# Values stationary and two heads side by side in the P.V product of two attentions, with 1/Z spread by TensorE

## The reference, cut to what matters

```
q, k, v = xn @ w_q, ctx @ w_k, ctx @ w_v          # per head 256x64, 512x64, 512x64
scores = q @ k.T * scale                          # layer 0: a score of 0 counts as -inf
attn = softmax(scores)                            # 256 x 512 for each batch and head
out = attn @ v                                    # 256 x 64
y = concat(out over 16 heads) @ w_out + b_out     # 256 x 1024 @ 1024 x 128
x = x + y                                         # layer 2: x + tanh(gate) * y
```

## Time and profile before

| | |
|---|---|
| median of 3 runs | 546.78 us (546.55 to 550.07) |
| the profiled execution's span | 545.7 us |
| its own time | not given apart from the span |
| PE, DVE, ACT, POOL busy | 92%, 79%, 63%, 52% |
| PE in P.V (L524) | 65.7 us in 1536 matmuls |
| PE in transposes of P (L509) | 82.0 us in 512 |
| PE in transposes of O (L536) | 10.2 us in 64 |

### The profile page before, as it was taken

How to read it: one execution, slowest core, us unless ns; L and a number is a source line. 1 busy time by engine, 2 the same in 40 slices (tenths; PEclk the granted TensorE clock), 3 DMA queues, 4 the chain that set the end, 5 groups by cost and what they waited for, 6 DMA issues and landing times. The chain is left out here.

```text
span 545.7 us, 13308 instructions
## 1 busy us (share of the span) xinstructions
PE 503.3 (92%) x4905; PEld 289.4 (53%) x4905; DVE 431.3 (79%) x1208; ACT 341.1 (63%) x683; POOL 282.0 (52%) x307
## 2 busy tenths in 40 slices
PE   7889999999899899998998899998999999999996
PEld 3345556667753233343334467635665556954574
DVE  7999999997585888736867899888777777587763
ACT  5698888888247366643762678638888888422212
POOL 7957777777834734400110943227888888400100
PEclk9999999999999899999999899999999999999999
DMA  8660000001130000000000221000000002000000
GB/s 226 141 176 14 1 2 3 1 2 41 40 117 0 2 0 2 3 1 0 2 1 21 78 78 58 2 1 1 2 3 1 1 3 79 2 0 1 2 0 20
DMA packets 24084, 15.43 MB, mean 28 GB/s; under 512 B 8083, under 2 KB 22230, under 8 KB 23894
## 3 DMA queue, kind: packets, MB, share of 16 engines
q1 hardware_dynamic: 24022, 14.60, 9.4%
HBM read 14.33 MB, written 0.26 MB: 27 GB/s over the span
## 5 line engine op out<-in xcount | busy, mean ns | idle before, releaser
L509 PE MATMUL pspair<-ident,PP 128*128 128x128 f32 x512 | 82.0, 283 | 2.0 <-ACT PP L1342 1.8
L509 PEld LDWEIGHTS pspair<-ident,PP 128*128 128x128 f32 x512 | 54.2, 141 | 29.7 <-issue 20.1
L524 PE MATMUL psO<-V,PP 128*128 128x64 f16 x1536 | 65.7, 193 | 2.6 <-DVE Oall L1751 2.0
L524 PEld LDWEIGHTS psO<-V,PP 128*128 128x128 f16 x1536 | 59.9, 98 | 9.1 <-DVE PP L1717 2.9
L1717 DVE TENSOR_TENSOR PP<-pspair,PP 128x512 f16<-128x512 f32 x64 | 44.0, 688 | 25.7 <-ACT PP L1326 25.7
L1405 ACT ACTIVATE PP<-pspair 128x1024 f32<-128x1024 f32 x48 | 46.5, 1021 | 25.4 <-PE pspair L709 25.3
L2401 POOL TENSOR_TENSOR ln_rs<-ln_ve,minus_half 128x4 f32<-128x4 f32 x10 | 10.3, 1032 | 84.2 <-DVE ln_ve L1608 81.0
L1342 ACT ACTIVATE PP<-scores_m,nm 128x512 f32<-128x512 f32 x64 | 46.5, 727 | 5.4 <-DVE nm L1701 5.4
L2412 POOL TENSOR_TENSOR PP<-acc,one 128x512 f16<-128x512 f32 x32 | 33.3, 1040 | 29.3 <-ACT acc L1324 29.3
L2412 POOL TENSOR_TENSOR PP<-y_sb,one 128x512 f16<-128x512 f32 x32 | 33.3, 1040 | 16.9 <-ACT y_sb L1324 16.9
L2415 POOL TENSOR_TENSOR PP<-y_sb,PP 128x512 f16<-128x512 f32 x32 | 37.2, 1161 | 2.5
(11 more groups left out here) (596 smaller groups left out, 1261.2 us busy)
## 6 DMA issues: line engine op xcount, KB each, us to landing
W<-in_L_ffn_W SPq DMA_DIRECT2D x16, 256.0 KB, 2.8
bigw<-in_L_xattn_w_q SPq DMA_DIRECT2D x2, 512.0 KB, 6.4
bigw<-in_L_xattn_w_kv SPq DMA_DIRECT2D x1, 1024.0 KB, 4.7
V<-in_ctx SPq DMA_DIRECT2D x1, 512.0 KB, 4.8
bigw<-in_L_xattn_w_v SPq DMA_DIRECT2D x1, 512.0 KB, 6.2
mask_b<-in_mask_BxS_ff SPq DMA_DIRECT2D x1, 512.0 KB, 7.6
bigw<-in_L_xattn_w_k SPq DMA_DIRECT2D x1, 512.0 KB, 5.8
bigw<-in_L_xattn_w_o SPq DMA_DIRECT2D x1, 512.0 KB, 3.9
```

What stands on the lines that cost most here:

```text
L509: mm = pe.transpose(bank[f"T{j % 2}"][:, k * P:(k + 1) * P], Pb[j % 4][:, k * P:(k + 1) * P], ident[:])
L524: mm = pe.matmul(bank["O"][:, (j % UPH) * a.dv:(j % UPH + 1) * a.dv], (PTH, PTL)[ppart][j % 4][:, k * P:(k + 1) * P], (VH, VL)[vpart][:, b ...
```

## The change

P.V is now computed once for each group, two units after the group's last one (at j%4=2), with the values stationary: for one head a block of 128 keys x 64 value columns is loaded, and the transposed probabilities of both query tiles (256 columns) move. The result has the head's 64 features on the partitions and 256 queries in the columns, so it comes out turned. The two heads of the pair use the lower and the upper 64 columns of the array, and so partitions 0 to 63 and 64 to 127 of bank O; their matmuls alternate (24 matmuls, `values`). The probabilities are kept for eight units in place of four; the further four buffers lie in `bigw`, where the oT buffers were.

1/Z now has to lie along the columns. `factors` makes it with four f32 matmuls for each group, into the other half of bank O: the stationary operand is one column of 1/Z repeated 64 times and the identity moves. ACT copies the result to `RT` (at j%4=3), and DVE multiplies O by RT at j%4=1, straight into `OT` in `Oall`. The transposes of O and the copies behind them are gone.

The output sums of pairs 0 to 5 are taken in the last eight units, one pair with each of j=8 to 13, all four token tiles accumulated in bank M (opened by a matmul of zeros); pair 6 comes behind the last unit, pair 7 in two halves around the last group's P.V, which is taken head by head. The last unit is split by DVE and no longer by POOL. DVE adds y to X in one instruction. Layer 0: the bias and `mask_prep` stand between the last unit's split and the last scaling. Layer 2: the 14 steps of the weight's quantisation and the bias go one by one into the last round's units. POOL's `selectors` wait for the output sums of pair 5.

```diff
-        PT = [PP[:, 4 + k, :] for k in range(4)]
-        PTH = [PT[k][:].bitcast(F16)[:, 0:SK] for k in range(4)]
-        PTL = [PT[k][:].bitcast(F16)[:, SK:2 * SK] for k in range(4)]
+        PT = [PP[:, 4 + k, :] for k in range(4)] + [bigw[:, k // 2, k % 2 * SK:(k % 2 + 1) * SK] for k in range(4)]
+        PTH = [PT[k][:].bitcast(F16)[:, 0:SK] for k in range(8)]
+        PTL = [PT[k][:].bitcast(F16)[:, SK:2 * SK] for k in range(8)]
+        PT_of = [t.rearrange("p a c -> p (a c)").bitcast(F16).rearrange("p (q h m c) -> p h m q c", q=2, h=2, m=2)
+                 for t in (PP[:, 4:8, :], bigw[:, 0:2, :])]
         VH = V[:, 0:4, :].rearrange("p a c -> p (a c)").bitcast(F16).rearrange("p (k c) -> p k c", k=NC)
         VL = V[:, 4:8, :].rearrange("p a c -> p (a c)").bitcast(F16).rearrange("p (k c) -> p k c", k=NC)
...
         minus16 = G[:, 0, 0, :].bitcast(F16)
-        OT = [bigw[:, c // 2, c % 2 * TOK:(c % 2 + 1) * TOK] for c in range(6)] + [kT1[:, 0:TOK], kT1[:, TOK:2 * TOK]]
+        OT = [O[:, (3, 1, 2, 0)[c // 2], c % 2 * TOK:(c % 2 + 1) * TOK] for c in range(NPAIR)]
...
                 mm.then_inc(full[b], 1)
 
-        def out_chunk(j):
-
...
-            def values(i, j):
-
-                if j % 2:
-                    pe.wait_ge(sem(f"{n}.split"), affine(i, j, UPI, 2) + 1)
...
+            def value_part(i, g, h, qs):
+
                 for k in range(a.kt):
+                    for m in range(len(PARTS)):
+                        mm = value_step(i, g, h, qs, k, m)
+                return mm
+
+            def value_step(i, g, h, qs, k, m):
+
+                (ppart, vpart), b, col = PARTS[m], g % B, (PPI * i + g // B) * P + h * DH
+                return pe.matmul(bank["O"][h * DH:(h + 1) * DH, qs.start * P:qs.stop * P]
+                                 .rearrange("p (q x) -> p q x", x=P),
+                                 (VH, VL)[vpart][:, b * a.kt + k, col:col + DH],
+                                 PT_of[g % 2][:, h, ppart, qs, k * P:(k + 1) * P],
+                                 start=(k == 0 and m == 0), stop=(k == a.kt - 1 and m == 2))
+
+            def values(i, g):
+
+                pe.wait_ge(sem(f"{n}.split"), 2 * (i * GPI + g) + 2)
+                emptied(pe, f"{n}.T0", 2 * (i * GPI + g) + 1)
+                reuse(f"{n}.O", i * GPI + g)
+                for k in range(a.kt):
+                    for m in range(len(PARTS)):
+                        for h in range(2):
+                            value_step(i, g, h, slice(0, 2), k, m)
+
+            def factors(i, g, ps, done):
+
+                pe.wait_ge(sem(f"{n}.rz"), i * GPI + g + 1)
+                for q in range(2):
+                    for h in range(2):
+                        mm = pe.matmul(ps[h * DH:(h + 1) * DH, q * P:(q + 1) * P],
+                                       rZ[:, g % 2, 2 * q + h:2 * q + h + 1].broadcast_to([P, DH]), ident[:],
+                                       start=True, stop=True)
+                mm.then_inc(done, 1)
 
             def out_sums(c, ts=range(NT)):
-                emptied(pe, f"{n}.oT{c}")
+
+                emptied(pe, f"{n}.O", B * c + ts[-1] // 2)
                 for t in ts:
-                    out_sum(t, c)
+                    mm = pe.matmul(bank["M"][:, t * P:(t + 1) * P], OT[c][:, t * P:(t + 1) * P], W(c),
+                                   start=False, stop=(c == NPAIR - 1 and t == NT - 1))
+                return mm
...
-                    if not (first and j < a.lag):
-                        values(*shift(i, j - a.lag))
+                    if j % UPH == 2 and not (first and j < UPH):
+                        group = (i, j // UPH - 1) if j >= UPH else (i - 1, GPI - 1)
+                        values(*group)
+                        factors(*group, bank["O"][:, S:2 * S], full["O"])
...
-                    if last and out_chunk(j) is not None:
-                        out_turn(out_chunk(j))
-                    if last and j >= UPI - 3:
-                        if j == UPI - 3:
-                            pe.wait_ge(sem(load), 16)
-                        for c in range(2):
-                            out_sums(c, [j - UPI + 3])
+                    if last and j == UPP:
+                        pe.wait_ge(sem(load), 16)
+                        take(pe, f"{n}.y", "M")
+                        pe.matmul(bank["M"], zero16[:], ident16[:].unsqueeze(1).broadcast_to([P, 4, P]),
+                                  start=True, stop=False)
+                    if last and UPP <= j < UPP + NPAIR - 2:
+                        mm = out_sums(j - UPP)
+                        if a.mask and j == UPP + NPAIR - 3:
+                            mm.then_inc(sem(f"{n}.summed"), 1)
 
...
             run(pe, a, rounds)
-            nr = a.units // UPI
...
+            i, g = a.units // UPI - 1, GPI - 1
+            out_sums(NPAIR - 2)
+            factors(i, g, take(pe, f"{n}.RT", "S0"), full["S0"])
+            reuse(f"{n}.O", i * GPI + g)
+            emptied(pe, f"{n}.T0", 2 * (i * GPI + g) + 1)
+            value_part(i, g, 0, slice(0, 2))
+            pe.wait_ge(sem(f"{n}.split"), 2 * (i * GPI + g) + 1)
+            value_part(i, g, 1, slice(0, 1))
+            out_sums(NPAIR - 1, range(0, 2))
+            emptied(pe, f"{n}.T1", 2 * (i * GPI + g) + 1)
+            value_part(i, g, 1, slice(1, 2)).then_inc(full["O"], 1)
+            out_sums(NPAIR - 1, range(2, 4)).then_inc(full["M"], 1)
...
-                if j % 2:
-                    if not isinstance(i, int) or i * UPI + j >= 4:
+                if not own_low(i, j, a):
+                    if i * UPI + j >= 4:
 
...
-                nc.scalar.copy(PTH[j % 4][:, 0:a.keys], ps[:, 0:a.keys]).then_inc(sem(f"{n}.high"), 1)
+                nc.scalar.copy(PTH[j % 8][:, 0:a.keys], ps[:, 0:a.keys]).then_inc(sem(f"{n}.high"), 1)
+
+            def factors(i, g):
+
+                filled(act, f"{n}.O", i * GPI + g)
+                nc.scalar.copy(RT[:], bank["O"][:, S:2 * S]).then_inc(sem(f"{n}.factors"), 1)
...
+                    if j % UPH == 3 and not (first and j < UPH):
+                        factors(*((i, j // UPH - 1) if j >= UPH else (i - 1, GPI - 1)))
...
             run(act, a, rounds)
+            emptied(act, f"{n}.O", a.units // UPH - 2)
+            act_copy(act, f"{n}.RT", RT[:], S)
...
+                    else:
+                        emptied(dve, f"{n}.RT")
+                    b = g % B
+                    dve.tensor_tensor(OT[PPI * i + g // B][:, b * S:(b + 1) * S], ps[:, 0:S], RT[:], ALU.mult)\
+                        .then_inc(free["O"], 1)
 
                 def rounds(i, first, last):
                     for j in range(UPI):
                         more = not (last and j >= UPP)
                         end = UPI if last else UPI + 4
                         group = (i, j // UPH - 1) if j >= UPH else (i - 1, GPI - 1)
-                        if j % 4 == 3 and not (first and j < UPH):
-                            norm(*group)
+                        if j % 4 == 1 and not (first and j < 2 * UPH):
+                            norm(*((i, j // UPH - 2) if j >= 2 * UPH else (i - 1, GPI - 2 + j // UPH)))
                         if j % UPP == 4 and more:
                             query_low(*pair(i, j // UPP + 1))
                         if a.mask:
@@ -1782,8 +1796,8 @@
                             evac(i, j)
                         if j % UPP == 7 and not last and not a.mask:
                             key_low(*pair(i, j // UPP + 2))
-                        if last and out_chunk(j) in a.dve_turns:
-                            copy(f"{n}.oT{out_chunk(j)}", OT[out_chunk(j)])
+                        if last and j < len(steps):
+                            steps[j]()
 
                 if a.mask:
...
-                norm(*group)
+                i = a.units // UPI - 1
+                recip(i, GPI - 1)
+                norm(i, GPI - 2)
+                evac(i, UPI - 1)
+                for step in behind:
+                    step()
+                norm(i, GPI - 1)
 
             def packed(a, last=(), behind=()):
...
-                weights[-1]().then_inc(sem("L2f.wq"), 1)
-                dve.wait_ge(sem("L2f.wq"), 1)
-                dve.wait_ge(sem("L2x.tanh"), 1)
-                link(dve.scalar_tensor_tensor(out=X[:], in0=wide(rowp["L2_xattn_b_out"]), scalar=tanh_g[:], in1=X[:],
-                                              op0=ALU.mult, op1=ALU.add))
-                for t in range(NT):
-                    ps = filled(dve, f"L2x.y{t}")
-                    dve.scalar_tensor_tensor(out=X[:, t, :], in0=ps[:, 0:P], scalar=tanh_g[:], in1=X[:, t, :],
-                                             op0=ALU.mult, op1=ALU.add).then_inc(free_of(f"L2x.y{t}"), 1)
-                for t in range(NT):
-                    emptied(dve, f"L2x.y{t}")
+                def with_bias():
+                    dve.wait_ge(sem("L2f.wq"), 1)
```

(21 more changed lines are left out.)

102 lines of the change are left out of this document (23 added, 79 removed).

## The result

The changed kernel takes 562.4 us (median of 5 runs, 561.0 to 568.7). The kernel before took 546.8 beside it. The ratio is 1.030, with a 95% interval of 1.026 to 1.034: slower, and outside the forecast range of 543 to 560.

A forecast was written before the change was run, and what follows sets the result against it. Bounds: DVE in layer 0, with an equally long ring; in layer 2 a ring through POOL's key split. +5.4 +2.7 +1.1 +1.5 -4.1 -3.1 = +3.5 us on 545.7 gave 549.2, median 550.3; range 543 to 560.

The forecast's parts named there:

- P.V and the factors: Each group on PE: P.V 1.28 us, factors 0.44, change of mode 0.11; 1.85 taken, 0.4 more than before.
- layer 0's steady part: Layer 0's wide attention: period 14.15 us in place of 13.76, DVE no longer the bound; +2.7 us over seven pairs.
- three legs: PE's period: scores to P.V, to the transpose at j%8=5, to the next scores; layer 0 before: 2.16, 5.60, 6.00 us.
- The sum: All stretches of the kernel: terms adding to +3.5 us on the span of 545.7, so 549.2; median 550.3.
- Layer 2's steady part: Layer 2's wide attention: period 13.94 us, +0.77, with PE waiting some 0.5 for POOL's split; +5.4 over seven pairs.
- ring: Layer 2's bound: scores wait for POOL's key split, through P.V, transpose, ACT's copy and POOL's splits; period 13.17 us before.
- The last pairs: Unit 8's transpose to unit 15's: 14.0 us, +1.1 in layer 0 and +1.5 in layer 2.
- The ends: Unit 15's transpose to the LayerNorm: layer 0 9.0 us, -3.1; layer 2 7.2 us, -4.1.
- sign: Ends of the attentions: the prediction is wrong if an end does not shrink by 3 us.
- The waits add up in layer 0: Rival: PE's gaps for DVE and ACT stay, layer 0's period 14.6 us, time 555; chance 0.23.
- rival of uncovered loads: P.V's 64-column loads not covered, 1.0 us more a group, 578 us; or halves in turn, 598; chance 0.10.
- The third rival: P.V itself gets shorter: half the time, 0.72 us a group, total 541.3 us; chance 0.04.

The follow-up runs named there:

- bunched run: Kernel before, old P.V, a group's four units issued together behind the third unit's turn, except each attention's last two groups: ratio 1.007.
- late, with pairs: Changed kernel, P.V and factors behind the fourth unit's turn, layer 2's maxima and exponentials by pairs, 11 filler matmuls in layer 0's end: 550.0 us.
- late order: Changed kernel with a group's P.V and factors moved behind the fourth unit's turn, one unit later: 557.2 us.
- cheaper factors: Late, pairs, filler kernel, 1/Z repeated over 64 columns, spread by two plain transposes, not four f32 matmuls: 574.5 us (turned), 572.1 (repeated by a copy).
- repeated factors: Late, pairs, filler kernel, four-column reciprocal repeated by a copy, two plain transposes: 572.1 us; the other kernel, with layer 2's second keys copied earlier: 569.0.
- keys first: Late, pairs, filler kernel with 1/Z turned by plain transposes, and layer 2's POOL key split ahead of the fifth unit's split: 570.5 us.

## Why the prediction was wrong

**P.V and the factors (right, but for one piece).** 1.85 us was forecast for a group, 1.87 measured; the halves do run side by side, 12 pairs in 1.34 us, where one after the other would take 2.56 by the prediction's 0.107 us a matmul. The parts are 1.34 (forecast 1.28, with 0.11 more for the change of mode) and 0.53 (0.44). The turn just ahead of a group is 0.09 longer, and that was missed: a group costs 0.54 more than before, not 0.4.

**The step that failed is layer 0's steady part.** The prediction wrote: "PE's wait for DVE goes, PE being later". It took the wait for a gap that added work fills. But the two units' P.V that stood beside DVE's chain were moved out of it, so the wait grew from 0.38 to 0.95. In the prediction's own three legs (from the scores to P.V, to the turn at j%8=5, to the next such scores), in the changed kernel's timeline:

```profile
74.10 0.82 PE L496 MATMUL psS<-Amat,Qst 64*128 64x512 f16 x6
76.15 1.50 PE L524 MATMUL psO<-bigw,V 128*64 128x256 f16 x24
83.08 1.09 PE L510 MATMUL pspair<-ident,PP 128*128 128x128 f32 x8
89.36 0.82 PE L496 MATMUL psS<-mask_b,Qst 64*128 64x512 f16 x6
```

The legs measure 2.05, 6.93 and 6.28 us where 2.16, 5.99 and 6.00 were put. The middle one is off by 0.94, which is the wait. The last one, kept at 6.00 without a reason, is 0.28 longer. The period was to rise by 0.39 and rose by 1.50: 0.36 by the bunching alone, 1.14 by the work (the bunched run against before and after). The sum was 6.0 us short here.

**Layer 2's steady part had the wrong ring.** The prediction let PE wait 0.5 us for POOL's split ahead of each second group and kept POOL's key split as the bound. Neither showed: P.V starts without a wait, and the scores wait for ACT. The legs are 1.78, 6.23 and 6.50 us (404.21, 405.99, 412.22 and 418.72 in PE's timeline) against 2.24, 5.78 and 5.92: the first has no wait, the second has one of 0.36 and the longer turn, the third the other of 1.01. +0.77 was forecast, +1.34 came. In the order in which that chain is covered (late, with pairs) POOL is again what ends PE's wait, and the period of 13.86 is near the 13.94 forecast. That is luck in part, since the wait of 0.5 us ahead of P.V is not there either. The forecast priced the form; it did not price the order in which it was put. 3.1 us short.

**The last pairs** (between unit 8's turn and unit 15's) were 0.6 and 0.4 us short. The rows show 0.1 at each of two turns ahead of P.V, and a sum behind the factors takes 1.09 and not 0.89; the rest is open. **The ends** were right: -2.8 and -4.1 against -3.1 and -4.1, though layer 0's stays short of the 3 us that the prediction set as a sign.

**Not seen at all:** the mask ahead of the last scaling leaves PE idle for 2.73 us, and the clock that falls after it costs the feed-forward 2.4 us. The prediction had counted the casts on DVE, and not asked what PE does meanwhile.

**The rivals.** "The waits add up in layer 0" was the right one in kind, at 0.23, and too small: it stopped at a period of 14.6 and 555 us, since it too took gaps for things that stay, not grow. The Trainium skill, TensorEngine Tiling (Array Packing), Restrictions, says that column tiling switches Fast Weight Load off. The loads of 64 columns are indeed no cheaper than those of 128 before, but the loads of the two halves lie over each other in time (408 loads of 110 ns fill 22.0 us, not 44.9), a pair keeps a pace of 0.111 us, and so the rival of uncovered loads did not come:

```profile
L524 PEld LDWEIGHTS psO<-bigw,V 128*64 128x64 f16 x408 | 22.0, 110 | 2.6 <-POOL bigw L2434 2.1
```

The third rival, a P.V of half the time, did not come either: 1.34 us a group against 1.42 for the four units before.

What stays open: whether layer 0 can keep its late order with cheaper factors, and why layer 0's start and first pairs differ between kernels by a few tenths; and why the cast of the mask took twice as long at its new place.

## What to carry to other kernels

Work that stands between two others in an in-order queue is also their cover: before gathering it into one block, ask of each place that it leaves which chain on other engines ran beside it, and put the block beside the longest. A wait in the profile is slack only if what causes it does not move with the change. And after a change that lets a nearly full TensorE idle for two or three microseconds, price the half clock that may follow, not the idle time alone.

## What the runs showed of the hardware

- VectorE's reciprocal of 256 columns took 1.73 us (6.8 ns a column), that of 4 columns 0.17, and its multiply of 256 columns 0.41: here it belongs on the few values, ahead of any repeat. The Trainium skill, VectorE: DVE Perf Modes, says under "First, the fixed hardware budget" that the reciprocal is an iterated divide with a repeat count of 8; the row agrees with it in kind (4.2 times the multiply), and no run here shows the factor by itself.
- The granted clock went to its lower level (1.2 GHz) after 2.73 us without work on TensorE at the end of layer 0. With the repeated factors it did so after four of six waits of 1.98 to 1.99 us in one kernel and two of six in the other, and stayed at 2.4 GHz after the rest; of two waits of 2.36 and 2.37 us, one in each, it fell after the first alone. Single waits of 0.95 and 1.01 us in the changed kernel's steady parts left it at 2.4 GHz, but with the keys first it fell once in layer 0 behind two waits of 0.61 and 1.07 us that stood 1.7 us apart.
- A turn just ahead of matmuls in column halves took 0.58 us to their start and not 0.49; 12 pairs of column halves of 256 columns ran at 0.111 us a pair, where 256 columns at 2.4 GHz are 0.107.
- GpSimd repeats four values over 256 columns in 0.61 us.
